# A one-core language-model tower: order of masks and sums in the first scan, and the way of the late weights through the prologue

## What is computed

```python
h = embed(x) * sqrt(192) + pe
# mixer on layernorm(h): u = rmsnorm(.)
zxbcdt = u @ in_proj_w                                   # z | xBC | dt
dt = softplus(zxbcdt[..., -N_HEADS:] + dt_bias)
xBC = silu(conv4(xBC) + conv_b)                          # x | B | C
def step(h, t):
    h = dec[..., None, None] * h + (dtt[..., None] * xt)[..., None] * bt[:, None, None, :]
    y = einsum('bhpn,bn->bhp', h, ct)
y = (y + D * xh).reshape(B, L, D_INNER) * silu(z)
h2 = y @ out_proj_w
v = rmsnorm(h2, norm2_w)
m = silu(v @ w_gate) * (v @ w_up) @ w_down
h = h + h2 + m
# experts on layernorm(h): top 2 of 8, and a shared one
y = einsum('tei,edi,te->td', silu(x @ w1) * (x @ w3), w2, cw)
z = silu(x @ sw1.T) * (x @ sw3.T) @ sw2.T
h = h + y + z
```

## Time and profile before

| what | value |
|---|---|
| median of 3 runs | 946.04 us (945.28 to 946.13) |
| the profiled execution | 945.58 us, span 943.7 us |
| TensorE busy | 838.4 us (89%) |
| VectorE, ScalarE, GpSimd busy | 671.2, 541.8 and 307.9 us |
| mean granted TensorE clock | 0.974 of full speed |

### The profile page before, as it was taken

One profiled execution on the slowest core, in us unless ns is written; L12 is line 12 of the kernel. 1 busy time (PEld: TensorE's weight loads), 2 busy tenths in 40 slices (PEclk: granted clock), 3 DMA queues, 4 the chain that ended last, 5 costly groups with the idle time before them and its releaser, 6 DMA issues.

```text
span 943.7 us, 22884 instructions
## 1 busy us (share of the span) xinstructions
PE 838.4 (89%) x7312; PEld 671.6 (71%) x7312; DVE 671.2 (71%) x1677; ACT 541.8 (57%) x1209; POOL 307.9 (33%) x447
## 2 busy tenths in 40 slices
PE   4647999999999999999999999999999999999858
PEld 3426777776777777777777777777777777777646
DVE  5476777768677776867768686876868687786524
ACT  4644665656566565656656565765656566664422
POOL 3334332423333242433324243332324333332202
PEclk9777999999999999999999999999999999999988
DMA  8500000000000000000000000000000000000000
GB/s 252 138 4 10 2 22 2 7 16 0 20 0 20 0 5 16 0 20 0 20 0 5 16 3 18 0 20 0 7 13 3 18 0 20 0 13 2 10 1 9
DMA packets 17107, 16.77 MB, mean 18 GB/s; under 512 B 6322, under 2 KB 15416, under 8 KB 16824
## 3 DMA queue, kind: packets, MB, share of 16 engines
q1 hardware_dynamic: 17080, 16.43, 6.1%
HBM read 12.23 MB, written 4.19 MB: 17 GB/s over the span
## 4 chain that ended last, share of the span: by engine, by line
PE 43%; issue 22%; DVE 13%; POOL 9%; ACT 4%; DVEq 1%; POOLq 1%; ACTq 0%
PE bank L1324 19%; POOL w_raw L540 5%; PE bank L1505 5%; DVE mr L1037 4%; PE bank L1550 4%; PE bank L1635 3%; PE bank L1481 2%; PE bank L1539 2%; POOL w_raw L537 2%; PE bank L1330 2%; DVE w_raw L1235 2%; PE bank L1577 2%; PE bank L1530 1%; POOL r L438 1%; PE bank L1332 1%
## 5 line engine op out<-in xcount | busy, mean ns | idle before, releaser
L1037 DVE SCALAR_TENSOR_TENSOR mr<-er,gm 128x512 f32<-128x512 f32 x192 | 130.4, 714 | 27.1 <-ACT er L728 24.9
L728 ACT ACTIVATE er<-bank 128x512 f32<-128x512 f32 x192 | 105.7, 596 | 49.9 <-PE bank L1481 44.5
L800 ACT ACTIVATE sg<-bank 128x256 f32<-128x256 f32 x144 | 55.2, 384 | 132.1 <-PE bank L1324 132.1
L1635 PE MATMUL bank<-w2t,w_raw 128*128 128x192 f32 x576 | 120.6, 332 | 4.3 <-DVE w_raw L1235 1.7
L979 DVE SCALAR_TENSOR_TENSOR xa<-xr,cw_,xa 128x256 f32<-128x256 f32 x192 | 113.7, 595 | 4.7 <-ACT xa L647 0.8
L540 POOL TENSOR_TENSOR w_raw<-w_raw 128x384 f32<-128x384 f32 x64 | 67.4, 1053 | 110.9 <-ACT w_raw L789 110.9
L1505 PE MATMUL bank<-mr,xd 128*32 128x128 f32 x1536 | 86.3, 285 | 19.1 <-DVE mr L1037 19.1
L1635 PEld LDWEIGHTS bank<-w2t,w_raw 128*128 128x128 f32 x576 | 90.1, 190 | 14.8 <-DVE w_raw L1235 10.0
L759 ACT ACTIVATE sg<-bank 128x256 f32<-128x256 f32 x96 | 36.8, 383 | 109.9 <-PE bank L1324 109.9
L1324 PE MATMUL bank<-x_h,w_hi 128*128 128x256 f16 x288 | 79.7, 277 | 21.6 <-DVE w_raw L1204 19.9
L1204 DVE TENSOR_TENSOR w_raw<-sg,bank 128x256 f32<-128x256 f32 x144 | 60.0, 417 | 41.1 <-ACT sg L800 40.2
(11 more groups left out here) (229 smaller groups left out, 2202.9 us busy)
## 6 DMA issues: line engine op xcount, KB each, us to landing
out<-w_raw SPq DMA_DIRECT2D x16, 192.0 KB, 2.0
w_raw<-weights SPq DMA_DIRECT2D x1, 1924.0 KB, 10.3
wt_raw<-weights SPq DMA_DIRECT2D x2, 962.0 KB, 15.9
pos<-position SPq DMA_DIRECT2D x16, 96.0 KB, 2.8
ri<-exponent_rows SPq DMA_DIRECT2D x4, 384.0 KB, 4.6
tok<-tokens SPq DMA_DIRECT2D x16, 70.0 KB
sums<-lj SPq DMA_DIRECT2D x16, 64.0 KB, 2.2
ri<-sums SPq DMA_DIRECT2D x64, 12.0 KB
```

The source lines that it names most:

```text
L728: act.activation(er[:, r % NER], p_d[r % 2][:].rearrange("p (h i) -> p h i", h=HG), ACT.Exp)\
L800: act.activation(sg[:, e % 2, :], p_pair[e % 2][:, 0:NB * Q], ACT.Silu).then_inc(sx_ready, 1)
L1037: ve.scalar_tensor_tensor(mr[:, r % NER], er[:, r % NER], 1.0, gm[:, b, :].unsqueeze(1).to_broadcast([128, HG, Q]), ALU.min, ALU.mult)\
L1635: ins = pe.matmul(p_out[(e + 1) % 2][:, b * D:(b + 1) * D], hh[:, e % NHH, b * Q:(b + 1) * Q], w2t[:, e, :], start=True, stop=True)
```

## The change

It has five parts.

1. In every first scan ACT does the fourth and fifth `er` ahead of `mixed_norm` (before, the fifth stood behind it); DVE does the fourth mask ahead of `t1`, `pre_onehot` one mask later, and `mixed` (`hm`) after `split_v`. PE's wait for `hm` moves from the start of `swiglu` to its first down product.
2. SP: `wo`, `wd` and `w2t` are loaded after `sums_in_rows(0)`.
3. PE's prologue: half of `project_in_x(1)`, exponents 0 and 1, the other half, exponents 2 and 3, the first scan, and only then `project_in_z(1)`. ACT's copies for the convolution of chunk 1 stand later in the scans.
4. Middle weights: the high parts on POOL (a multiplication by a column of scales, ahead of `steps_decay(1)`), the low ones on DVE, one before the first scan of chunk 0 and one after the second. Last weights: the low parts as four pieces of 1156 columns on DVE in the MLP of body 0; none on POOL.
5. ACT loads its tables early by three small operations (`warm`), where it waits anyway.

```diff
@@ load_rest / ramp (SP)
+
+            def load_last():
                 sp.dma_start(wo[:], w_out).then_inc(in_late, 16)
                 sp.dma_start(wd[:], w_down).then_inc(in_late, 16)
                 sp.dma_start(w2t[:], w2).then_inc(in_late, 16)
...
                 sums_in_rows(0)
+                load_last()
                 sums_in_rows(1)
@@ GpSimd
+            def middle_weights():
+                m = slice(COL_G, COL_E)
+                pool.wait_ge(in_w, 64)
+                pool.wait_ge(in_mid, 48)
+                settle(pool)
+                pool.tensor_scalar(w_hi[:, m], w_raw[:, m], nrm[:, 2:3], None, ALU.mult).then_inc(w_rest_hi, 1)
+                pool.tensor_scalar(wt_hi[:, m], wt_raw[:, m], nrm[:, 3:4], None, ALU.mult).then_inc(w_rest_hi, 1)
@@ ScalarE
+                act.wait_ge(setup_p, SETUP_P)
+                act.activation(warm[:, 1:2], mhalf[:, 0:1], ACT.Exp)
                 b_on_tokens(0)
                 decays(0)
-                scan(0, 0, {2: lambda: convolved_in(1, 0, p_out), 4: lambda: convolved_in(1, 1, p_out)})
-                setup_rest()
-                scan(0, 1, {})
+                scan(0, 0, {4: lambda: convolved_in(1, 0, p_out)})
+                scan(0, 1, {0: lambda: convolved_in(1, 1, p_out)})
                 operands(1, p_out[0])
+                act.activation(warm[:, 2:3], mhalf[:, 0:1], ACT.Silu)
...
-                    scan(f, 0, {3: lambda: mixed(b), 4: lambda: mixed_norm(b)})
+                    scan(f, 0, {3: lambda: mixed(b), 5: lambda: mixed_norm(b)})
@@ VectorE
-                    if q == (2, 5)[b]:
+                    if q == (3, 5)[b]:
...
+                    if not later(c) and t in (0, 2, 3, 5):
+                        last_weights(*divmod((0, 2, 3, 5).index(t), 2))
...
                 masked_g(0)
+                middle_weights(0)
                 scan(0, 0, {})
...
                 operands(1, p_out[0])
-                setup_rest()
+                middle_weights(1)
...
                 if f is not None:
-                    scan(f, 0, {3: mixed_and_tokens})
-                else:
-                    mixed(b)
+                    scan(f, 0, {} if p is None else {4: lambda: pre_onehot(p)})
                 split_v(b)
+                mixed(b)
@@ TensorE
-                project_in_x(1, p_out)
-                project_in_z(1, p_pair)
-                for r in range(4):
-                    exponents(0, r)
-                scan(0, 0, {})
+                project_in_x(1, p_out, (0, 1))
+                exponents(0, 0)
+                exponents(0, 1)
+                project_in_x(1, p_out, (2, 3))
+                exponents(0, 2)
+                exponents(0, 3)
+                scan(0, 0, {})
+                project_in_z(1, p_pair)
                 running_sums(1, p_out[0])
```

More of the change, by code:

```diff
@@ L546, in norm2, with last_weights @@
                 rsqrt(b, stat2_ready, mv2[:, :, 1], 1.0, 1e-5, var2[:], r2[:], front_p, 1, 1, r2_ready)
-            def last_weights(wt):
-                hi, lo, raw = (wt_hi, wt_lo, wt_raw) if wt else (w_hi, w_lo, w_raw)
-                x = slice(COL_E, COLS)
[L552 to L560, removed]
+            def middle_weights():
[5 more added lines that the diff above has]
+                pool.tensor_scalar(wt_hi[:, m], wt_raw[:, m], nrm[:, 3:4], None, ALU.mult).then_inc(w_rest_hi, 1)
+            def last_weights(hi, raw):
+                x = slice(COL_E, COLS)
+                pool.tensor_copy(hi[:, x], raw[:, x]).then_inc(w_last_hi, 1)
             def ramp():
@@ L588, in body @@
                     keep(f)
-                    if not later(b):
-                        last_weights(1)[1]()
                     gate(f, 0)
@@ L849, in ramp @@
                 gates(1, 0, p_pair)
+                act.activation(warm[:, 3:4], mhalf[:, 0:1], ACT.Exp)
                 b_on_tokens(1)
@@ L859, in body @@
                 split_v(b)
-                act.activation(warm[:], mhalf[:, 0:1], ACT.Silu)
+                act.activation(warm[:, 0:1], mhalf[:, 0:1], ACT.Silu)
                 swiglu(b, p)
@@ L1283, in body @@
             def body(p, f, b):
-                def mixed_and_tokens():
-                    if p is not None:
-                        pre_onehot(p)
-                    mixed(b)
                 if f is not None:
-                    scan(f, 0, {3: mixed_and_tokens})
-                else:
-                    mixed(b)
+                    scan(f, 0, {} if p is None else {4: lambda: pre_onehot(p)})
                 split_v(b)
+                mixed(b)
                 if f is not None:
@@ L1369, in project_dt, with project_in_x @@
                 ins.then_inc(dt_done, 1)
-            def project_in_x(c, dst=p_d):
+            def project_in_x(c, dst=p_d, tiles=range(4)):
                 pe.wait_ge(u_hi_ready, c + 1)
@@ L1379, in project_in_x @@
                         pe.wait_ge(e_ready, c * NR)
-                    else:
+                    elif dst is p_out:
                         pe.wait_ge(h0_ready, c + 1)
                 settle(pe)
-                for i in range(2):
-                    for j in range(2):
-                        col = COL_X + (2 * i + j) * 128
-                        ins = split_products(dst[i][:, j * NB * Q:(j + 1) * NB * Q], slice(col, col + 128),
-                                             u_h, u_l, slice(0, NB * Q), True)
-                    ins.then_inc(x_done[i], 1)
+                for t in tiles:
+                    i, j = divmod(t, 2)
+                    col = COL_X + t * 128
+                    ins = split_products(dst[i][:, j * NB * Q:(j + 1) * NB * Q], slice(col, col + 128),
+                                         u_h, u_l, slice(0, NB * Q), True)
+                    if j == 1:
+                        ins.then_inc(x_done[i], 1)
             def project_in_z(c, dst=(p_y, p_misc)):
@@ L1609, in experts @@
                 if not later(c):
-                    pe.wait_ge(w_last, 4)
+                    pe.wait_ge(w_last_hi, 2)
+                    pe.wait_ge(w_last_lo, 4)
                 pe.wait_ge(x_hi_ready, c + 1)
```

37 lines of the change are left out of this document (17 added, 20 removed).

## The result

The changed kernel takes **932.76 us** (median of 4 runs, 930.75 to 934.82), the kernel before 946.09 us in the same session (945.28 to 946.37): a ratio of 0.9865, 95% interval 0.9841 to 0.9888. That is 13.3 us less; the forecast was 12.0.

What follows compares the result with a forecast made beforehand. The loop's time was taken as PE's, the prologue's as waits for a DMA and VectorE's chain. Terms -6.3 - 3.2 - 4.8 + 2.3 = -12.0 us gave 934.0 us; range 929.5 to 939 to hold 8 in 10.

Steps and rivals of the forecast that it cites:

- 15 first scans: Bodies 0 to 14: PE's wait before the fourth mask's products goes, 0.42 us each, -6.3 us (0 to -7.0).
- start of the first scan of chunk 0: Prologue: exponents 0 come 5.2 us earlier, partly lost behind the weight preparation; -3.2 us (-6 to +0.5).
- from there to exponents (1, 0): Prologue, second scan onward: one low part fewer on VectorE, then `ri` is last; -4.8 us (-5.5 to -3.5).
- low parts in body 0: MLP of body 0: four VectorE pieces, 5.4 us, only partly fit idle time; +2.3 us (0 to 5.4).
- I count the wait as 0.42: First scans: PE's wait before the fourth mask, 0.36 us in its row, counted with 0.06 of record overlap.
- Rival 2: First scans: the turn waits for `vn`, the loop's gain is 0 and the prologue's 5.7 stay; 940 us, chance 0.10.
- the margin of 0.1 that I counted: First scans: `vn`, moved behind the fifth exponential, would be done about 0.1 us before the turn needs it.
- rival 1: Prologue: GpSimd's new operation is slow, 5.3 us each, or wins the port, masks queue behind it; 937.7 us, chance 0.17.
- I take 2.0, near the cast, whose width is nearest: Prologue: each of GpSimd's two middle high parts takes 2.0 us, between bounds of 1.4 and 5.3.
- The line on what the profile would show: Signs of being right, among them exponents 0 at 35, exponents (1, 0) near 66.5 and iterations shorter by 0.4 us.
- nothing waited for it in body 0: Body 0: removing GpSimd's 4.57 us for each low part gains nothing, as no engine waited for it.
- Rival 4: Prologue gives more: masks at their own pace, body 0 loses nothing, PE's clock full longer; 929 us, chance 0.10.

Runs made afterwards that it cites:

- experiment 6: Changed kernel with `mixed_norm` back ahead of the fifth exponential in the first scans: 930.75 us, ratio 0.9844 to the kernel before.
- experiment 4: Changed kernel with `t1` back ahead of the fourth mask on VectorE: 943.11 us, ratio 0.9974 to the kernel before.
- experiment 5: Changed kernel with the residual sum `hm` back ahead of the split and PE's wait for it at the MLP's start: 935.65 us.
- experiment 9: Changed kernel with GpSimd's two middle high parts as plain copies, without the norm's factor: 926.22 us.
- experiment 8: Changed kernel with the middle high parts on ScalarE and VectorE's first low part behind the first scan of chunk 0: 926.65 us.
- experiment 2: Changed kernel with the first scans' reordering (part 1) undone, leaving parts 2 to 5: 943.87 us, ratio 0.9976 to the kernel before.
- experiment 1: Kernel before with only part 1, the order of masks, norm and residual sum: 934.29 us, ratio 0.9883.
- experiment 3: Kernel before with only part 2, the loads of `wo`, `wd` and `w2t` behind `sums_in_rows(0)`: 941.28 us, ratio 0.995.
- experiment 10: Changed kernel with two of the four last-weight low parts moved from body 0's MLP into the prologue: 931.52 us.
- experiment 11: Changed kernel with middle high parts on ScalarE, `mixed_norm` ahead of the fifth exponential, and two low parts moved into the prologue: 923.00 us.
- experiment 12: Kernel of experiment 11 with `project_in_z(1)` also ahead of the first scan of chunk 0: 921.81 us.

## Why the prediction was right, and where by luck

The total was off by 1.2 us, its terms by much more:

| term | predicted | measured |
|---|---|---|
| 15 first scans | -6.3 | 15 x -0.71 = -10.6 |
| start of the first scan of chunk 0 | -3.2 | +2.45 |
| from there to exponents (1, 0) | -4.8 | -5.26 |
| low parts in body 0 | +2.3 | +1.48 |
| clock in body 0's first scan | not counted | -1.79 |
| from the last `rm` to the end | not counted | -1.34 |
| sum | -12.0 | -15.1 (profiled executions) |

**First scans: the mechanism right, the size wrong.** The step that failed is "I count the wait as 0.42". PE's own row says 0.36, but the ends of matmuls are modelled, and the row of the weight load shows more, in the kernel before:

```profile
469.76 0.36 PEld L1505 LDWEIGHTS bank<-mr,xd 128*32 128x32 f32 x8 [0.63 <-DVE mr L1037]
```

Idle was 0.63 us, and the pause had a second price. A group of eight behind a wait took 0.57 to the next matmul (469.76 to 470.33); without one, all sixteen take 0.59 (460.71 to 461.30 in experiment 6). From the third mask's first product to the turn it was 1.56 (468.77 to 470.33) and without waits it is 0.59, so the wait for the fourth mask was worth 0.97, and not 0.42. So the term's bound of -7.0 did not reach far enough. Of the 0.97 the turn's wait for `vn` takes 0.35 back (experiment 6), which leaves the 0.62 of experiment 4. Rival 2 was thus at work too: the margin of 0.1 that I counted was not there. I had `vn` ready 1.73 to 1.83 after exponents 4 and it is after 1.64 (461.58 - 459.94); but I had the turn at 1.89 (469.91 - 468.02), and it could come at 1.34 (experiment 6). The deadline moved, since the gain was larger. The gain of 0.05 that I allowed for a shorter wait ahead of the MLP is 0.10 (experiment 5).

**Start of the first scan: wrong, and rival 1 is the reason.** Exponents 0 come at 35.05, as predicted (35.1). The step that failed is "I take 2.0, near the cast, whose width is nearest": the product with a column of scales takes 4.17 us each, in the bounds of 1.4 and 5.3 and nearer to the upper one. The row of 48 columns with the same operation was the better witness than the cast of 2312 columns with another. Experiment 9 shows it (plain copies 1.47, the mask at 36.77), and experiment 8 gives the same by another way (ScalarE instead, the mask at 36.81): each saves 6 to 6.5 us. With mask 0 at 40.71 and not 36.1 the term is 4.6 worse, and the way from it to `state_share` took 11.1 against the 8.1 and 1.6 that I had, 1.4 more. (The two make 6.0 and not the 5.65 of the table, because I counted from the scan's end at 49.0 and the table from `state_share` at 49.38.) In the 1.4 are, among other things, two masks that took 3.84 us beside GpSimd's cast of 2.58 at 46.27:

```profile
45.55 3.84 DVE L1036 SCALAR_TENSOR_TENSOR mr<-er,gm 128x512 f32<-128x512 f32 x2 [0.50 <-ACT er L718]
```

The term's bound of +0.5 and rival 1's 937.7 don't follow from the prediction's own numbers either: a mask 0 near 42 is 5.9 later than the 36.1 of the term, which gives -3.2 + 5.9 = +2.7, and 939.9 for the rival. The measured +2.45 lies outside the bound as it was stated (and is +2.9 to +3.6 in the traces of experiments 2, 4, 5 and 6).

The Trainium skill (GPSIMD Engine Reference, section "3.1 Elementwise") states 1.03 cycles an element for bodies of at most two operations, 1.3 us here as an estimate. The copy's 1.47 is near to it, the product with a scale is three times that; the measurement decides.

**To exponents (1, 0): right in size and cause.** -5.26 against -4.8 (-4.5 to -5.2 in experiments 2, 4, 5 and 6), and `ri` ends the wait (1.73 us), issued at 73.44 and used at 76.51, 3.07 later. The line on what the profile would show gave exponents (1, 0) "near 66.5"; that doesn't follow from the terms, which give 79.32 - 3.2 - 4.8 = 71.3. It was an error of mine in that line alone.

**Low parts in body 0: right in kind.** +1.48 against +2.3. The pieces ran in 1.35, as taken from the rate, but one that met GpSimd's product took 1.87, and more of them fitted the gaps than I gave them. The 1.48 is against a step that no kernel ran (53.97). In experiment 2, with the old order, the pieces cost 55.78 - 54.68 = 1.10. And the reason "nothing waited for it in body 0" holds only for the old order: with the new one and GpSimd's product still in body 0, the step is 55.19 (experiment 1), so that the pieces cost 0.26 more than what they replace.

```profile
87.32 1.87 DVE L917 TENSOR_TENSOR w_lo<-w_raw,w_hi 128x1156 f16<-128x1156 f32 x1
93.42 1.35 DVE L917 TENSOR_TENSOR w_lo<-w_raw,w_hi 128x1156 f16<-128x1156 f32 x1
```

**Not foreseen: the clock.** Rival 4 named it for the whole prologue; it shows in one place. Windows over the matmuls from exponents (1, 0) to those before the first masks of body 0, before and after:

```profile
79.30:83.80 4.50, 4.48 (x16) 3.87 (x17) 1.75 (x3) 1.83 (x4) 0.00 (x0) 0.59 0.02 4
```

```profile
76.50:79.20 2.70, 2.69 (x16) 2.39 (x17) 1.52 (x3) 1.69 (x3) 0.00 (x0) 1.00 0.16 48
```

The same 16 records take 4.48 us at a granted clock of 0.59 (near the lower of the two levels, 1.2 GHz) and 2.69 at 1.00 (2.4 GHz). Before, PE had stood idle for 3.54 us until 71.04 and for 3.91 until 77.74, here waiting for `xd` behind the low parts, and the granted clock was 0.50 from 71 to 83. After, the waits are 2.45 us until 72.01 and 1.73 until 76.51, and the clock is 1.00 throughout:

```profile
77.74 1.01 PE L1465 MATMUL bank<-lj,spread 128*128 128x256 f16 x4 [3.91 <-DVE xd L1023]
```

The change does not give the clock back in every execution. The stretch takes 5.44 to 5.80 us in the three traces with the old order of the prologue's VectorE work (before, experiments 1 and 3) and 4.00 to 4.02 in ten of the eleven others, but 5.75 in that of experiment 10. The -1.34 after the last `rm` I don't count as the change's: this stretch lasted 45.6 to 48.2 us in the executions of kernels whose end is the same.

**The total came out right because two errors cancelled**: 4.3 us too little in the loop, 5.7 too much at the start of the prologue. Of the prologue the moved DMAs earn 4.7 (experiment 3), and parts 3 to 5 together lose 2.6 by the medians (1.4 by the traces). They were not run one by one. GpSimd's slow product accounts for more than that loss: with plain copies in its place the same parts are 6.5 us faster (experiment 9).

## What to carry to other kernels

A short wait of PE between small matmul groups is worth more than PE's row says: read the weight load's idle time and compare the whole stretch with one that has no wait. Take the duration of an operation from a row of the same operation, even a far smaller one, rather than from a wide row of another; before a weight preparation goes to GpSimd beside VectorE's masks, ask for ScalarE first. When a change has several parts, run each alone: here one part of the prologue earned more than all of them together.

## What the runs showed of the hardware that was not expected

- GpSimd, 128 x 1536, f32 to f16: a product with a per-partition scale takes 4.17 us (2.7 ns a column), a plain copy 1.47 us (0.96 ns a column). ScalarE does the same product in 1.58 us (experiment 11):

```profile
42.80 1.58 ACT L620 ACTIVATE w_hi<-w_raw,nrm 128x1536 f16<-128x1536 f32 x1
```

- A pause of 0.63 us in PE's weight loads cost 0.97 us on the way to the next work.
- VectorE's product of 1536 columns, 1.82 us alone, took 4.85 beside GpSimd's product and ended 0.74 after it, and four masks of 2.49 us took 4.83 beside a cast of 2.58. A mask beside POOL's power (128 x 2, 0.72 us) took its usual 0.69.
- Filling PE's wait early in the prologue (experiment 12) saved 1.06 us there. Then 0.77 went into a longer wait for VectorE, and two later windows ran at a granted clock of 0.79 and 0.66 instead of 0.94 and 1.00 and took 0.73 longer.
- A write of 64 KB and the reads that depend on it: from issue to issue 9.3 and 10.0 us with six weight transfers ahead in SP's queue (before, experiment 1), 4.0 to 5.5 with three (the other twelve traces), 2.3 with none (chunk 1).
